# A two-layer graph and expert kernel: the first layer's norms, router ranks, gates and unit passes put in another order, and two runs of filler products

## The reference

```python
def sensitivity(r, mu, sigma):
    return jnp.exp(-(1.0 / r - 1.0 / mu) ** 2 / (2.0 * sigma * sigma))   # mu 1, sigma 0.5

# layer 0, graph
weights = jnp.where(adj < 1.0, sensitivity(adj), 0.0)
x = x + weights @ (layernorm(x) @ W + B)
# layer 0, experts: 8 experts of width 256, two of them for each row
z = layernorm(x)
gate_logits = z @ Wg + bg + bias
topk_vals, topk_idx = top_k(gate_logits, 2)
combine = one_hot(topk_idx, 8) weighted by softmax(topk_vals)
h = relu(einsum('td,edh->teh', z, W1) + b1)
x = x + einsum('ted,te->td', einsum('teh,ehd->ted', h, W2) + b2, combine)
# layer 1, graph: signed attention over adj with 3 heads and two GRU cells
# layer 1, experts: 8 experts of width 341, silu(z @ w1) * (z @ w3) @ w2, two for each row
```

## Time and profile before

| | us |
|---|---|
| median of 3 runs | 506.44 (504.66 to 507.1) |
| the profiled execution | 505.56 |
| its span, first to last instruction | 503.8 |
| outside the span | 1.76 |
| TensorE busy | 434.5 (86%) |
| VectorE busy | 336.8 (67%) |
| ScalarE busy | 233.5 (46%) |
| mean granted TensorE clock | 0.954 |

### The profile page before, as it was taken

The page is one execution under the profiler, slowest core; times in us unless marked ns, Lnnn a source line. Parts: engine busy times, 40 slices in busy tenths (PEclk is TensorE's granted clock), DMA queues, the critical chain, the costliest instruction groups (busy, mean ns, idle before and its releaser), DMA issues.

```text
span 503.8 us, 6121 instructions
## 1 busy us (share of the span) xinstructions
PE 434.5 (86%) x1754; PEld 252.8 (50%) x1756; DVE 336.8 (67%) x729; ACT 233.5 (46%) x377; POOL 63.8 (13%) x112
## 2 busy tenths in 40 slices
PE   4678596987969989999989999999997869899996
PEld 2533362544536565454554343444444546668785
DVE  0997989786656774233576589597848845775572
ACT  4988869567968552303124312232032115644431
POOL 5000000000010000000000000010140332374333
PEclk9679678998989999999999999999999988999999
DMA  8989400000000100000000000072010012013142
GB/s 281 295 258 385 187 0 0 1 0 1 0 3 0 55 2 0 1 0 1 1 2 0 0 1 0 31 251 59 25 43 1 17 48 59 29 44 87 58 122 69
DMA packets 25356, 30.44 MB, mean 60 GB/s; under 512 B 3267, under 2 KB 19856, under 8 KB 25320
## 3 DMA queue, kind: packets, MB, share of 16 engines
q1 hardware_dynamic: 22711, 26.56, 16.5%
q0 software_dynamic: 1568, 2.92, 1.7%
q10 hardware_dynamic: 1040, 0.52, 0.4%
HBM read 19.73 MB, written 10.26 MB: 60 GB/s over the span
## 4 chain that ended last, share of the span: by engine, by line
PE 49%; DVE 27%; ACT 10%; issue 10%; POOL 2%; DMA 1%; SPq 0%; DVEq 0%; POOLq 0%; ACTq 0%
PE bank L1365 8%; PE bank L1179 5%; DVE pr_ring L2145 4%; PE bank L1444 4%; PE bank L1428 3%; PE bank L1429 3%; PE bank L1140 3%; PE bank L1313 2%; PE bank L1029 2%; DVE y_units L1571 2%; DVE y_units L1582 2%; PE bank L1435 2%; DVE t_units L1577 2%; PE bank L1354 2%; DVE hr_ring L1949 2%
## 5 line engine op out<-in xcount | busy, mean ns | idle before, releaser
L1365 PE MATMUL bank<-pr_ring,hW 128*128 128x512 f32 (+3 forms) x198 | 93.8, 558 | 9.2 <-DVE pr_ring L2145 8.2
L2145 DVE SCALAR_TENSOR_TENSOR pr_ring<-adjT,regR,bank 128x512 f32<-128x512 f32 (+3 forms) x99 | 63.9, 680 | 27.5 <-PE bank L1354 26.2
L1365 PEld LDWEIGHTS bank<-pr_ring,hW 128*128 128x128 f32 (+1 forms) x198 | 33.4, 190 | 42.6 <-DVE pr_ring L2145 28.5
L1029 PE MATMUL bank<-y_units,msg 128*128 128x512 f32 (+3 forms) x66 | 34.3, 652 | 17.3 <-DVE y_units L1592 17.3
L1949 DVE TENSOR_TENSOR hr_ring<-hr_ring,bank 128x512 f32<-128x512 f32 (+1 forms) x48 | 29.4, 620 | 22.8 <-ACT hr_ring L822 18.7
L1140 PE MATMUL bank<-hr_ring,W2s 128*128 128x512 f32 (+1 forms) x96 | 44.3, 548 | 0.0
L822 ACT ACTIVATE hr_ring<-bank,b1c 128x512 f32<-128x512 f32 (+1 forms) x48 | 29.8, 629 | 15.7 <-PE bank L999 15.7
L997 PE MATMUL bank<-zhi,W1hi 128*128 128x512 f32 (+1 forms) x48 | 34.9, 726 | 0.1
L598 POOL DMA_INDIRECT xg<-rowx,slot x22 | 22.2, 1010 | 64.8 <-DVE slot L1703 58.2
L1029 PEld LDWEIGHTS bank<-y_units,msg 128*128 128x128 f32 (+1 forms) x66 | 13.7, 221 | 30.9 <-DVE y_units L1592 21.9
L604 POOL DMA_INDIRECT yg<-pr_ring,goes x23 | 22.1, 963 | 44.3 <-DVE pr_ring L2174 43.4
(11 more groups left out here) (356 smaller groups left out, 867.8 us busy)
## 6 DMA issues: line engine op xcount, KB each, us to landing
xg<-zeros SPq DMA_DIRECT2D x1, 6110.0 KB
wall<-in_w SPq DMA_DIRECT2D x2, 1364.0 KB
adjT<-in_adjT SPq DMA_DIRECT2D x1, 2560.0 KB
xblk<-xg SPq DMA_DIRECT2D x30, 65.0 KB, 1.8
adjT<-in_adjT SPq DMA_DIRECT2D x1, 1650.0 KB
adjT<-in_adjT SPq DMA_DIRECT2D x3, 512.0 KB, 5.7
adjT<-in_adjT SPq DMA_DIRECT2D x1, 1024.0 KB
W1f<-in_W SPq DMA_DIRECT2D x1, 1024.0 KB, 11.9
```

Source lines behind the costliest of these rows:

```text
L1029: mm = nc.tensor.matmul(B_GNN[:, 0:w], msg[0:r, j, :], y_units[0:r, g % RINGY, i, 0:w], start=(j == 0), stop=(j == T - 1))
L1365: nc.tensor.matmul(B_ACC[:, 0:w], hW[0:r, j, k * P:(k + 1) * P], ring[0:r, 0:w], start=(k == 0 and j == 0), stop=(k == K - 1 and j == T - ...
L2145: nc.vector.scalar_tensor_tensor(out=pr_ring[0:r, 4 + p % R_RING, 0:w], in0=adjT[0:r, j, cols(c)], scalar=g_col[0:r, j, k:k + 1], in1=B_F[ ...
```

## The change

Seven edits. (1) `centred` is now true for norm 1 of all chunks and for norm 2 of chunk 2: four norms get the centred form, norm 1 with its product in bank 2 (the bank of the graph sums), norm 2 of chunk 2 in bank 1. So the sums of the next chunk must wait for the norm's last step. (2) The ranks of layer 0's router use three instructions in place of five; the constant `floor` is made by GpSimd at the program's start in place of `floor1` later. (3) Ahead of the loop VectorE scales chunk 0's norm and runs its router before `step` of unit 6; the `arg` and `exp` of unit 6, `cut` 6 and `mult` and `step` of unit 7 go into the loop. (4) `turn` stands ahead of the `exact` of tiles 2, 18 and 33 (a new table `PE0A`), and a chunk's first gate is made one tile later. (5) The three tables are written anew for tiles 0 to 31; the eleven `neg` stand behind tiles 23 to 33 in place of 14 to 33. (6) `keep(10)` ahead of chunk 0's logits becomes `keep(12)`. (7) At the seam `keep(10)` is new, and `mid(1, 2)` stands ahead of `block_turned(0)`.

```diff
+PE0A = {2: [("turn", 0)], 18: [("turn", 1)], 33: [("turn", 2)]}
 ACT0 = {
-    0: [("sq", 9), ("ln", 9), ("arg", 7), ("exp", 7), ("inv", 9)], 2: [("arg", 8), ("sq", 10), ("ln", 10), ("inv", 10)], 3: [("exp", 8)],
+    0: [("sq", 9), ("arg", 6), ("exp", 6)], 1: [("ln", 9), ("inv", 9)], 2: [("arg", 7), ("exp", 7), ("sq", 10)], 3: [("ln", 10), ("inv", 10)],
...
 def centred(l, c):
-    return l == 3 and c < C - 1
+    return l == 1 or (l, c) == (2, C - 1) or (l == 3 and c < C - 1)
...
+        def center_bank(l):
+            return bk[1] if l == 2 else bk[2]
...
                     if c == 0:
                         at(pe, "rows_dve", 2)
+                    else:
+                        at(pe, "ln_z", LN_AT[1, c - 1] + 1)
...
                 at(pe, "h_relu", q - 2)
+                for task in PE0A.get(q, []):
+                    side(task)
...
-                if e == 0 and m == 1:
-                    gate(q - 1)
-                elif e and m == 0:
+                if e == 1 and m == 0:
+                    gate(q - M0)
+                if e and m == 0:
                     gate(q)
...
-                link(nc.vector.tensor_tensor(g4[0], other, own, ALU.is_gt))
-                link(nc.vector.tensor_tensor(g4[1], other, own, ALU.is_ge))
-                link(nc.vector.tensor_tensor(g4[1], g4[1], tri[:, :, :].unsqueeze(1).to_broadcast([P, k, E, E]), ALU.mult))
-                link(nc.vector.tensor_tensor(g4[0], g4[0], g4[1], ALU.max))
-                link(nc.vector.tensor_reduce(G, g4[0], AX.X, ALU.add))
+                link(nc.vector.tensor_tensor(g4[0], X0.unsqueeze(2).to_broadcast([P, k, E, E]), X0.unsqueeze(3).to_broadcast([P, k, E, E]), ALU.subtract))
+                link(nc.vector.tensor_tensor(g4[1], g4[0], floor[:, :, :].unsqueeze(1).to_broadcast([P, k, E, E]), ALU.is_gt))
+                link(nc.vector.tensor_reduce(G, g4[1], AX.X, ALU.add))
...
             newton_product(6)
+            ln_scale(1, 0)
+            route(0)
             newton_step(6)
-            ln_scale(1, 0)
-            cutoff(6)
-            route(0)
+            turned(0)
             newton_sign(7)
-            turned(0)
-            newton_product(7)
-            newton_step(7)
...
                 last_gates()
+                keep(10)
...
+                gat_side(("mid", 1, C - 1))
                 block_turned(0)
-                gat_side(("mid", 1, C - 1))
```

More of the change, by code:

```diff
@@ L106 @@
-    28: [("var", 1, 2)], 30: [("logits", 2)], 32: [("htok", 0)], 33: [("turn", 2), ("hw", 0)], 34: [("hw", 1)], 35: [("hw", 2)], 36: [("hw", 3)],
+    4: [("unit", 6)], 5: [("v",)], 6: [("unit", 7)], 8: [("unit", 8)], 9: [("unit", 9)], 11: [("unit", 10), ("unit", 11)],
+    12: [("mean", 1, 1)], 13: [("var", 1, 1)], 15: [("logits", 1)], 16: [("unit", 12)], 19: [("unit", 13)], 20: [("mean", 2, 0), ("unit", 14)],
+    22: [("var", 2, 0), ("unit", 15)], 23: [("unit", 16)], 24: [("unit", 17)], 26: [("mean", 1, 2)],
@@ new lines @@
+    12: [("center", 1, 1), ("sq", 14)], 13: [("var", 1, 1), ("ln", 14)], 14: [("inv", 14)], 15: [("rank", 1), ("arg", 13), ("exp", 13), ("sq", 15)],
+    16: [("ln", 15), ("inv", 15)], 17: [("sq", 16), ("ln", 16), ("inv", 16)], 18: [("arg", 14), ("exp", 14)], 19: [("arg", 15), ("exp", 15), ("sq", 17)],
+    20: [("ln", 17), ("inv", 17)], 21: [("center", 2, 0), ("arg", 16), ("exp", 16)], 22: [("var", 2, 0), ("arg", 17), ("exp", 17)],
+    23: [("neg", 0), ("neg", 1)], 24: [("neg", 2)], 25: [("neg", 3), ("neg", 4)], 26: [("center", 1, 2)], 27: [("neg", 5)],
@@ L170 @@
 ALONE = 1
-CONSTS1 = 15
+CONSTS1 = 14
 KEEP = LATE - E
@@ L1123, in _ @@
             side(("var", 1, 0))
-            keep(10)
+            keep(12)
             pe.wait_ge(s["ffn0_in"], 80)
@@ L1551, in ln_scale @@
                 at(dve, "ln_y0", n + 1)
-                nc.vector.scalar_tensor_tensor(out=xc, in0=B_XC[:, 0:w] if centred(l, c) else xc, scalar=-0.5, in1=y, op0=ALU.mult, op1=ALU.mult).then_inc(s["ln_step"], 1)
+                nc.vector.scalar_tensor_tensor(out=xc, in0=center_bank(l)[:, 0:w] if centred(l, c) else xc, scalar=-0.5, in1=y, op0=ALU.mult, op1=ALU.mult).then_inc(s["ln_step"], 1)
                 at(dve, "ln_y2", n + 1)
```

57 lines of the change are left out of this document (22 added, 35 removed).

## The result

| | before | changed |
|---|---|---|
| median | 505.97 us (504.66 to 507.1, 4 runs) | 486.12 us (485.43 to 486.6, 4 runs) |
| profiled execution, its span | 505.56, 503.8 | 485.43, 483.7 |
| TensorE busy | 434.5 (86%) | 427.7 (88%) |
| mean granted clock | 0.954 | 0.982 |

The ratio is 0.9596, with a 95% interval of 0.9558 to 0.9635: the changed kernel is faster by 4%. The forecast was 488.5 us, with a range of 482.5 to 498.

The account below looks back on a forecast made before the run. From 62.4 to 150.1 us no engine is full; VectorE and ScalarE wait for each other. Gains of 3.9 and 14.7 less 2.5 give 16, plus 2 at the seam: 18 from 505.56, 487.6; median 488.5 us, range 482.5 to 498.

Parts of the forecast that it names:

- the ring: Gates' copy to x1(2): VectorE and ScalarE wait for each other; 73 us in place of 87.7, 14.7 us won.
- The walk through the queues: Three engine queues followed tile by tile up to x1(2): x1(1) near 90.8, x1(2) near 129.5, VectorE 4.6 us idle.
- the sum: The forecast's count of work and gains by stretch: 16 us up to the loop's end plus 2 at the seam.
- The start: Ahead of and at the loop's start: chunk 0's gates' copy ends at 58.45 in place of 62.38, 3.9 us sooner.
- The 4.49 us wait: TensorE ahead of chunk 2's last units: blamed on `neg` 2 and layer 1's norm running ahead of a relu.
- Given back: Behind tile 23: nine `neg` between relus 23 and 31 fill ScalarE for 19.9 us; 2.5 us lost again.
- The centred norms: Norms read from PSUM: 0.72 us sooner at the start, 0.69 less VectorE work for chunk 1, reads cost nothing.
- The turn: `turn` ahead of the `exact` of tile 2: lets it run during the gates' copy; alone worth nothing.
- The seam: Behind the attention's last gates: fillers and the moved `mid(1, 2)` keep the clock; 2 us, ends 0 and 2.85.
- Half open: Rival in the loop: costlier handovers and queued `neg` lose half of 14.7 us and one at the seam; 496.8; chance 0.20.
- slower: Rival up to x1(2): TensorE's many small rests keep its clock at 0.50; 547 us; chance 0.03.
- Closes entirely: Rival in the loop: VectorE at its 66.5 us floor, ScalarE's `neg` block overlapped; 5 us more, 483.5; chance 0.13.

Follow-up runs that it names:

- old_order: The changed kernel with the loop's unit, norm and negative-part passes in the order of the kernel before; 503.36 us, ratio 0.9933.
- neg_new: The kernel before with only the eleven negative-part passes moved to behind tiles 23 to 33; 505.86 us, ratio 0.9986.
- neg_old: The changed kernel with the eleven negative-part passes back behind tiles 14 to 33; 485.4 us, ratio 0.9574.
- no_seam_tail: The changed kernel without both seam edits, and with GpSimd's last additions waiting for VectorE's last joiner tile; 487.72 us.

## Right and wrong, point by point

- **The bound.** Right: the ring of VectorE and ScalarE limited up to x1(2). The walk through the queues gave x1(1) at 90.8 and x1(2) at 129.5; they began at 90.18 and 128.65. From the copy's end the stretch took 70.2 us, where the walk gives 71 and the forecast, with 2 us for misfits, 73. VectorE was busy for 64.89 of them, not for the 66.5 that the sum took as its floor, and idle for 5.3, where the walk had 4.6 and the forecast 6.6. So the work was counted 1.6 us too high and the idle 1.3. This term, 17.5 where the sum had 14.7, is most of what was missing. Its idle fell where the walk put it: 0.56 and 0.59 us for the gates of chunk 1, and 2.39 for one relu, that ahead of x1(2):

```profile
128.04 0.69 DVE L1945 TENSOR_TENSOR hr_ring<-hr_ring,bank 128x512 f32<-128x512 f32 x1 [2.39 <-ACT hr_ring L824]
```

The forecast named a wait of over 2 us as a sign of being wrong; this one was in its walk already. "No pause over 1.3 us" on TensorE was not quite so: one of 1.54 stands ahead of the sums at 80.09, and the clock held.

- **The start.** Right in size, 3.95 for 3.9, but the pieces that the forecast names (1.8, 0.9 and 0.9) add up to 3.6. Measured are 1.83 (the scaling began at 50.19), 1.14 for `cut` 6 and the logits, and 0.91 for the ranks; the centred norm cost 0.73 and the ranks 0.93 when undone alone. Wrong in what it is worth: "a microsecond won ahead of tile 25 moves everything behind it" holds for the new order; in old_order 3.30 us of it came to 0.89 at the loop's end.
- **The 4.49 us wait and the `neg`.** Wrong. The forecast laid it to the `neg` and the norm ahead of the relu. Moving the `neg` alone (neg_new) brought 2.46 of the 21.5 us at x1(2), putting them back (neg_old) cost 1.53. What did it is the order of the unit and norm passes. That each engine now asks for the result of the round before fits the waits, 14.9 down to 6.3 us, but no run changes that alone.
- **Given back.** Right: 2.17 for 2.5, with nine `neg` between the relus of tiles 23 (124.07) and 31 (142.26) as one block on ScalarE; it took 18.9 us to the end of relu 31, where the sum had 19.9. That relu is 19.4 us sooner where 16.1 was forecast, most of the difference being the ring's. Not foreseen was what stands behind it: the pause at tile 33 is 1.61 us and close to costing the clock, as three versions showed that moved it by some tenths.
- **The centred norms.** At the start as forecast, and reading them from a bank cost nothing (VectorE 0.69 us, ScalarE 0.60). For norm 1 of chunk 2 the sum had no term; without the centred form the part behind x1(2) is 1.36 us longer, more than the 0.73 at the start or the 1.07 in the ring.
- **The turn.** "Alone worth nothing": so measured, 485.99 against 486.12.
- **The seam.** Right: about 2 us. The clock shows no 0.50 behind it, and the idle was 0.46, 0.77 and 0.42 us around the first blocks.
- **Unforeseen.** 0.55 us were lost at the end, by the collision. Another 0.73 were lost in the graph part of layer 1 by a spell of low clock. That belongs to this execution and not to the change: no_seam_tail, with the same code up to there, has none. Here the forecast had luck: in the profile the two hid 1.28 us of what the ring brought beyond it.
- **The rivals.** Half open and slower did not come. "Closes entirely" put x1(2) at VectorE's floor, 66.5 us behind the copy; it took 70.2, between that and the 73.

## What to carry to other kernels

Where two in-order queues serve each other, write down for each engine which round's result each instruction asks for; an order laid out so that all ask for the result of the round before closed a ring here with no less work, and was worth 17 of 20 us. Behind such a gain look for the next place where an engine arrives early: here a lead of 1.3 us turned into a loss of 0.6, since it made a pause at which the clock fell, and five filler products with a copy moved ahead turned it back. A single profile should be split at fixed instructions before its parts are compared, as the whole hid a loss of up to 4 us at the very end.
